# Layer 1: turned tiles in four PSUM banks where the experts' two are idle, in two elsewhere

## The chip, the cores and the metric

The kernel runs on one core of a Trainium2 chip. Its time is the device time in microseconds (us), the median of three runs. The engines are TensorE (PE; its weight loads are shown apart, as PEld), VectorE (DVE), ScalarE (ACT), GpSimd (POOL) and SyncE (SP), which issues transfers. PSUM, into which TensorE writes, is used here as eight banks of 128 partitions x 512 fp32 values.

## What is computed

Two transformer layers with adaptive layer norm on x of 8 x 512 x 128. Layer 0 is attention through landmarks with an iterated inverse, then a mixture of experts with capacity. The change lies in layer 1. Its part of the reference, cut:

```
h = _layernorm(x) * (1 + ca) + sa
# attention a = 0: 16 heads of 8, a bias by distance, gated
scores = einsum('bhqd,bhkd->bhqk', q, k) * scale + _tisa_bias(...)
attn = einsum('bhqk,bhkd->bhqd', softmax(scores), v)
a, g = split(attn @ w_gate + b_gate);  x = x + ga * (a * sigmoid(g))
h = _layernorm(x) * (1 + cb) + sb
# attention a = 1: causal, keys and values through a latent of 64
h = h + mla(rmsnorm(h, g1), Wq, Wdkv, Wuk, Wuv, Wo)
# 8 experts of 128 -> 256 -> 128, the two best weighted by a softmax
h = h + moe(rmsnorm(h, g2), gate_w, w1, w2)
x = x + gb * h
```

(The residual sums inside belong to the second block; each token's logits choose two experts, but all eight are computed.)

## The kernel before

**Tiles and steps.** Layer 1 works through 16 passes (`ORDER`): for each of the 8 sequences one pass of attention a = 0 and one causal pass a = 1, interleaved. A pass has 64 tiles, each 128 queries of one head against the keys: 512 of them for a = 0, and 128, 256, 384 or 512 for a = 1. The 1024 tiles (`ALL`) are software-pipelined: every engine runs one loop over steps m and does its part of a tile with a fixed lag. There is no scheduler; the order on each engine is what these loops write.

**A tile's way.** TensorE computes scores of tile m+2 into one of three banks (0 to 2, line 1723). VectorE adds bias or mask, negates and takes the minimum (line 1900, `X`, `nmax`; three buffers). GpSimd forms the difference to the row maximum (line 1583, `Y`; four buffers). TensorE turns tile m-3 of `Y` into a PSUM bank, one transpose per 128 keys (line 1737). ScalarE reads it from there through an exponential into `PT` (line 1625). Every fourth step TensorE multiplies four tiles of `PT` by the values into bank 5 (line 1752); the last column gives the sum for the softmax.

**Turned tiles and their slots.** Not only `Y` goes through the turned banks, but everything that TensorE makes for ScalarE to move: the output `O` of four heads (line 1762, every 16 steps), its turning for the projection (`turn`, 1766), the gate's two tiles (1772), the normalised rows (`xp`, `xm`, `xf`, 1778), projections (`pq`, `pk`, `mq` 1783; `ml` 1785; `mk` 1788) and values (`pv`, `mv` 1792). `turn_slots` numbers all 1200 of them in the order of the program, `SLOT[what]`. Slot c uses bank 3 + c % 2. Before TensorE writes one it waits until ScalarE has moved slot c - 2 (semaphore `moved`); ScalarE waits for `turned`. `moved` and `turned` count in slot order.

**The experts.** A round of experts (`moe`) runs beside the tiles for one sequence, at the steps `MOE_START[b]` and the 68 after: first the projection by Wo into bank `SIDE` (6), logits into bank `SIDE2` (7), then for each of 8 experts the hidden matmuls (line 1832) and the output ones (line 1846) in both banks; VectorE adds the outputs up (line 2095, semaphore `ye_added`). The rounds begin at steps 250, 378, 506, 634, 762, 890, 979 and 1043; the last one uses banks 0 to 2 for what comes before the outputs. Between rounds banks 6 and 7 are idle. The a = 0 passes are the first and those at odd places up to the 13th; nearly every one of them also carries the middle of a sequence (`mid`: gate, residual, two norms; on VectorE at places 22 to 36 of the pass).

**Waits.** TensorE works strictly in order: an instruction that waits holds up all behind it, so a transpose held by `moved` also holds the score matmul that VectorE needs next.

Of the kernel before, what the change touches and what calls it, by code (L numbers as in the profile page):

```python
# [13 lines left out]
B = 8  # L14
T = 512
# [9 lines left out]
E = 8  # L25
# [1215 lines left out]
TILES = H * TT  # L1241
# [5 lines left out]
ALL = len(ORDER) * TILES  # L1247
# [6 lines left out]
MOE_START = {b: TILES * PLACE[1, b + 1] - 6 for b in range(B - 2)}  # L1254
MOE_START[B - 2] = TILES * PLACE[1, B - 1] + MID_AT + 1
MOE_START[B - 1] = TILES * len(ORDER) + MID_AT + 1
HALVES = 2

STAGES = dict(wo=1, add=3, square=4, power=5, scale=7, turn=10, logits=12, read=14, top0=15, top1=16, gap=18,
              combine=20, first=12, each=6, second=2, tanh=1, mul=2, ye=9, half=2, sum=2)  # L1260
# [27 lines left out]
STEPS = MOE_START[B - 1] + done_at(B - 1) + 1  # L1288
# [1 line left out]
X_BUFS, Y_BUFS, PT_BUFS, W_BUFS, VW = 3, 4, 2, 3, HD + 2  # L1290
GATHER_AT, PRE_AT = 40, 2
T_LAG = 3
SIDE, SIDE2 = 6, 7


def tile_of(n):
# [8 lines left out]
def moe_at(m):  # L1305

    return [(b, m - first) for b, first in MOE_START.items() if 0 <= m - first <= done_at(b)]
# [7 lines left out]
def turned_at(s, i):  # L1315

    found = []
    if s < 0:
        return [("xp", 0), ("pq", 0), ("pk", 0), ("pv", 0)] if i == TILES - 1 else []
    if i % GROUP == 13 and 4 * s + i // GROUP >= 1 and 4 * s + i // GROUP <= 4 * len(ORDER):  # L1320
        found.append(("O", 4 * s + i // GROUP - 1))
    if i == MID_AT and 0 < s <= len(ORDER):
        found.append(("turn", s - 1))
    if s in MID_OF:
        found += [(name, MID_OF[s]) for at, name in ((19, "gate0"), (20, "gate1"), (38, "xm"), (40, "mq"), (41, "ml"),
                                                      (44, "mk"), (45, "mv")) if i == at]
    if s in PRE_OF:
        found += [(name, PRE_OF[s]) for at, name in ((10, "xp"), (21, "pq"), (23, "pk"), (25, "pv")) if i == at]
    found += [("xf", b) for b, k in moe_at(s * TILES + i) if k == stages(b)["turn"]]
    return found  # L1330


def turn_slots():

    slots = {}
    for m in range(-TILES, STEPS):
        if 0 <= m - T_LAG < ALL:
            slots["T", m - T_LAG] = len(slots)
        for what in turned_at(*divmod(m, TILES)):
            slots[what] = len(slots)  # L1340
    return slots


SLOT = turn_slots()


def layer1_phase(nc, sb_, sem, ps, x_sb, ident, half, mod_col, mods_dram, bias_dram, parts_dram, gate_keep,
# [4 lines left out]
    with local:  # L1352
# [79 lines left out]
        moved = sem("moved")  # L1432
# [17 lines left out]
        ye_added = sem("ye_added")  # L1450
# [20 lines left out]
        with nc.Block() as block:  # L1471
# [135 lines left out]
            def _(act):  # L1607
# [3 lines left out]

                def bank(what):
                    act.wait_ge(turned, SLOT[what] + 1)
                    return ps[:, 3 + SLOT[what] % 2, :]

                def move(n):
                    a, b, g, q, h = tile_of(n)
# [94 lines left out]
            def _(pe):  # L1712
# [11 lines left out]
                                     stack[:, 1, h, 0:keys(a, q)], start=True, stop=True).then_inc(scores_ready, 1)  # L1724

                def bank(what):
                    c = SLOT[what]
                    if c >= 2:
                        pe.wait_ge(moved, c - 1)
                    return 3 + c % 2  # L1730

                def transpose(n):
                    a, b, g, q, h = tile_of(n)
# [23 lines left out]
                def turn(name, k):  # L1757
# [34 lines left out]
                            last = nc.tensor.matmul(ps[:, to, t * C:(t + 1) * C], src[:, t * P:(t + 1) * P], w, start=True, stop=True)  # L1792
                    last.then_inc(turned, 1)

                def moe_side(b, i):
                    p = stages(b)
                    if i == p["wo"]:
                        if b == B - 1:
                            pe.wait_ge(shifted, ALL)
                        elif b:  # L1800
                            pe.wait_ge(ye_added, b * E * HALVES)
                        pe.wait_ge(moved, SLOT["turn", PLACE[1, b]] + 1)
                        for t in range(TT):
                            last = nc.tensor.matmul(ps[:, side_bank(b), t * C:(t + 1) * C], oT[1][:, t * P:(t + 1) * P], Wo_sb[:],
                                                    start=True, stop=True)
                        last.then_inc(mla_ready, 1)
                    if i == p["logits"]:
                        pe.wait_ge(moved, SLOT["xf", b] + 1)
                        for t in range(TT):
                            last = nc.tensor.matmul(ps[:, logits_bank(b), t * E:(t + 1) * E], fT[:, t * P:(t + 1) * P], gate_w_sb[:],  # L1810
                                                    start=True, stop=True)
                        last.then_inc(l1_logits, 1)
                    for e in range(E):
                        n = b * E + e
                        for f in range(FT1):
                            if i == hidden_at(b, e, f):
                                if f == 0:
                                    pe.wait_ge(experts_loaded[n % W_BUFS], (n // W_BUFS + 1) * 32)
                                if b == B - 1:
                                    if e == 0 and f == 0:  # L1820
                                        pe.wait_ge(mla_read, b + 1)
                                    elif e == 1 and f == 0:
                                        pe.wait_ge(logits_read, b + 1)
                                    elif e >= 1:
                                        pe.wait_ge(hid_evac, n * FT1 + f - 2)
                                elif e == 0:
                                    pe.wait_ge((mla_read, logits_read)[f], b + 1)
                                elif e == 1:
                                    pe.wait_ge(hid_evac, (n - 1) * FT1 + f + 1)
                                else:  # L1830
                                    pe.wait_ge(ye_added, (n - 2) * HALVES + f + 1)
                                nc.tensor.matmul(ps[:, hidden_bank(b, e, f), :], w1_e[:, n % W_BUFS, f * P:(f + 1) * P], fT[:],  # L1832
                                                 start=True, stop=True).then_inc(hid_ready, 1)
                        for u in range(HALVES):
                            if i == ye_at(b, e, u):
                                if u == 0:
                                    pe.wait_ge(hid_evac, (n + 1) * FT1)
                                if b == B - 1:
                                    pe.wait_ge(ye_added, (n - 1) * HALVES + u + 1)
                                elif e < E - 1:  # L1840
                                    pe.wait_ge(hid_evac, (n + 1) * FT1 + u + 1)
                                else:
                                    pe.wait_ge(ye_added, (n - 1) * HALVES + u + 1)
                                for t in (2 * u, 2 * u + 1):
                                    for f in range(FT1):
                                        last = nc.tensor.matmul(ps[:, SIDE + u, t * C:(t + 1) * C], hid[:, e % 2, f, t * P:(t + 1) * P],  # L1846
                                                                w2_e[:, n % W_BUFS, f, :], start=(f == 0), stop=(f == FT1 - 1))
                                last.then_inc(ye_ready, 1)
# [315 lines left out]
```

## Time and profile before

| | |
|---|---|
| median of three runs | 2079.36 us (2076.03 to 2079.79) |
| the profiled execution | 2073.5 us |
| its span, first to last instruction | 2071.5 us |
| TensorE busy, share of the span | 1779.4 us, 86% |
| its weight loads | 1306.9 us, 63% |
| VectorE | 1444.1 us, 70% |
| ScalarE | 1015.6 us, 49% |
| GpSimd | 857.9 us, 41% |
| granted clock of TensorE, mean over the span | 0.943 |

Layer 1's tiles run from 752 us to the end. Shares over the span mix layer 0 with layer 1, so the prediction reads single stretches. "Busy" adds up the shown durations; matmuls are pipelined, so TensorE's pace is better read from the starts of its instructions than from their lengths (a transpose of four matmuls has a shown length of 0.60 us, but the next instruction can start 0.44 us after it).

### The profile page before, as it was taken

What the parts mean: (1) busy time and instruction counts of PE and PEld (TensorE: products, weight loads), DVE (VectorE), ACT (ScalarE), POOL (GpSimd) and SP (SyncE); (2) the same over time, 40 slices, a digit from 0 to 9 for tenths busy, and PEclk for the clock granted to TensorE, in tenths of its full rate; (3) what the DMA queues carried; (4) which work ended last, traced back from release to release, by engine and by line L of the source; (5) the groups of instructions that cost most, each with busy time, mean ns of one, the idle gap of its engine ahead of it and who ended that gap; (6) DMA issues with size and microseconds to landing.
All of it is one profiled execution on the core that took longest, in us unless ns stands there. A gap on an engine that the chain in (4) does not pass through costs nothing.

```text
span 2071.5 us, 56863 instructions
## 1 busy us (share of the span) xinstructions
PE 1779.4 (86%) x21284; PEld 1306.9 (63%) x21284; DVE 1444.1 (70%) x4537; ACT 1015.6 (49%) x1992; POOL 857.9 (41%) x1253
## 2 busy tenths in 40 slices
PE   4485898898875729999999999999999999999997
PEld 2374677677763517766667666667666667766665
DVE  4574778876761127777787786787886887778765
ACT  1252544455441206666655654654654555655542
POOL 3500101110013017767655654655754663664530
PEclk7797999999996959999999999999999999999998
DMA  2512211222006411012013012012012112111211
GB/s 94 166 24 72 76 42 51 61 75 74 7 6 208 142 67 39 33 57 77 17 71 96 11 69 87 21 72 86 26 66 85 32 60 83 35 54 40 83 32 48
DMA packets 102694, 131.72 MB, mean 64 GB/s; under 512 B 14448, under 2 KB 87536, under 8 KB 101272
## 3 DMA queue, kind: packets, MB, share of 16 engines
q1 hardware_dynamic: 70600, 98.59, 14.6%
q10 hardware_dynamic: 28496, 18.10, 3.0%
q0 software_dynamic: 3328, 11.40, 1.7%
q8 instruction: 173, 2.83, 0.6%
q14 instruction: 97, 0.79, 0.1%
HBM read 100.05 MB, written 28.15 MB: 62 GB/s over the span
## 4 chain that ended last, share of the span: by engine, by line
PE 45%; DVE 8%; issue 6%; DMA 5%; POOL 2%; ACT 1%; ACTq 1%; SPq 1%; POOLq 0%; DVEq 0%
PE ps L1737 13%; PE ps L1752 7%; PE ps L1723 6%; PE ps L1846 5%; PE ps L1832 4%; DMA l_w_e<-in_L_ffn_w_dram 2%; DVE l_X L1900 2%; DMA l_stack<-parts_dram 2%; PE ps L1199 1%; POOL l_Y L1583 1%; PE ps L1208 1%; PE ps L1762 1%; PE ps L1783 1%; DVE l_xn L1931 1%; ACT PT L1625 1%
## 5 line engine op out<-in xcount | busy, mean ns | idle before, releaser
L1583 POOL TENSOR_SCALAR l_Y<-l_X,l_nmax 128x512 f32<-128x512 f32 (+3 forms) x1024 | 674.6, 664 | 521.1 <-PE ps L1737 286.0
L1625 ACT ACTIVATE PT<-ps 128x512 f32<-128x512 f32 (+3 forms) x1024 | 520.0, 517 | 405.8 <-PE ps L1737 356.3
L1737 PE MATMUL ps<-ident,l_Y 128*128 128x128 f32 x3328 | 549.7, 280 | 11.7 <-ACT PT L1625 7.7
L1737 PEld LDWEIGHTS ps<-ident,l_Y 128*128 128x128 f32 x3328 | 387.2, 142 | 195.3 <-issue 82.4
L1900 DVE CUSTOM_DVE_ANT_0 l_X<-ps,strips 128x512 f32<-128x512 f32 x512 | 342.1, 687 | 134.2 <-PE ps L1723 130.9
L1723 PE MATMUL ps<-l_stack 72*128 72x512 bf16 (+3 forms) x1024 | 351.0, 345 | 66.9 <-DVE l_nmax L1900 50.0
L1900 DVE CUSTOM_DVE_ANT_0 l_X<-ps,mask 128x384 f32<-128x384 f32 (+3 forms) x512 | 238.5, 485 | 41.0 <-PE ps L1723 35.6
L1752 PE MATMUL ps<-PT,v_aug 128*10 128x128 f32 x6656 | 230.1, 274 | 0.0
L1752 PEld LDWEIGHTS ps<-PT,v_aug 128*10 128x10 f32 x6656 | 156.8, 91 | 71.5 <-ACT PT L1625 42.6
L1723 PEld LDWEIGHTS ps<-l_stack 72*128 72x128 bf16 x1024 | 102.0, 100 | 102.6 <-DVE l_nmax L1900 77.3
L1832 PE MATMUL ps<-l_fT,l_w_e 128*128 128x512 f32 x256 | 138.9, 631 | 12.1 <-DMA l_w_e<-in_L_ffn_w_dram 9.3
L2084 DVE SCALAR_TENSOR_TENSOR l_hid<-l_hid,ps 128x512 f32<-128x512 f32 x128 | 87.7, 686 | 83.0 <-ACT l_hid L1689 81.6
L1846 PE MATMUL ps<-l_w_e,l_hid 128*128 128x128 f32 x1024 | 139.9, 281 | 3.1 <-DVE h_tok L2095 1.7
L1846 PEld LDWEIGHTS ps<-l_w_e,l_hid 128*128 128x128 f32 x1024 | 126.2, 192 | 21.7 <-issue 16.6
L512 POOL DMA_INDIRECT slots_in<-h,slot_all x32 | 32.4, 1014 | 230.3 <-DVE slot_all L1078 223.0
L1689 ACT ACTIVATE l_hid<-ps 128x512 f32<-128x512 f32 x128 | 76.3, 597 | 90.3 <-PE ps L1832 90.3
L668 PE MATMUL ps<-AV,Q 64*64 64x128 f32 (+1 forms) x1280 | 84.3, 289 | 36.0 <-DVE Q L1097 35.9
L480 POOL TENSOR_TENSOR rstd<-var_eps,half 128x4 f32<-128x4 f32 x16 | 17.8, 1111 | 232.3 <-DVE var_eps L864 232.3
L668 PE MATMUL ps<-X,AV 64*64 64x64 f32 x2560 | 93.1, 223 | 19.1 <-DVE X L1097 18.5
L2095 DVE SCALAR_TENSOR_TENSOR h_tok<-ps,combine,h_tok 128x128 f32<-128x128 f32 x256 | 77.3, 345 | 43.4 <-PE ps L1846 42.9
L668 PEld LDWEIGHTS ps<-X,AV 64*64 64x64 f32 x2560 | 82.7, 137 | 31.7 <-issue 16.4
L668 PEld LDWEIGHTS ps<-AV,Q 64*64 64x64 f32 x1280 | 74.6, 150 | 42.8 <-DVE Q L1097 40.0
(276 smaller groups left out, 2508.6 us busy)
## 6 DMA issues: line engine op xcount, KB each, us to landing
stack<-parts_dram SPq DMA_DIRECT2D x48, 384.0 KB
l_stack<-parts_dram SPq DMA_DIRECT2D x64, 288.0 KB
l_stack<-parts_dram SPq DMA_DIRECT2D x192, 96.0 KB
l_w_e<-in_L_ffn_w_dram ACTq DMA_DIRECT2D x128, 128.0 KB, 2.2
parts_dram<-l_parts SPq DMA_DIRECT2D x32, 384.0 KB, 2.5
strips<-bias_dram POOLq DMA_DIRECT2D x16, 448.0 KB, 11.2
parts_dram<-parts SPq DMA_DIRECT2D x16, 384.0 KB, 10.9
w_e<-in_L_ffn_w_dram SPq DMA_DIRECT2D x12, 256.0 KB, 5.7
```

The source lines that it names most:

```text
L668: last = nc.tensor.matmul(out(h), lhs(h), rhs(h), start=True, stop=True)
L1583: nc.gpsimd.tensor_scalar(Y[:, n % Y_BUFS, 0:w], X[:, n % X_BUFS, 0:w], -1.0, nmax[:, n % 8:n % 8 + 1], ALU.mult, ALU.add).then_inc(y_pool, 1)
L1625: nc.scalar.activation(dst, src, ACT.Exp).then_inc(moved, 1)
L1689: nc.scalar.activation(hid[:, e % 2, f, :], ps[:, hidden_bank(b, e, f), :], ACT.Tanh, scale=0.5).then_inc(hid_tanh, 1)
L1723: nc.tensor.matmul(ps[:, n % 3, 0:keys(a, q)], stack[:, 0, h, q * P:(q + 1) * P], stack[:, 1, h, 0:keys(a, q)], start=True, stop=True).the ...
L1737: last = nc.tensor.transpose(ps[:, to, k * P:(k + 1) * P], Y[:, n % Y_BUFS, k * P:(k + 1) * P], ident[:])
L1752: last = nc.tensor.matmul(ps[32 * j:32 * j + VW, 5, q * P:(q + 1) * P], v_aug[PLACE[a, b] % 2][:, k, h + j, :], PT[:, unit % PT_BUFS, j, k ...
L1832: nc.tensor.matmul(ps[:, hidden_bank(b, e, f), :], w1_e[:, n % W_BUFS, f * P:(f + 1) * P], fT[:], start=True, stop=True).then_inc(hid_read ...
L1846: last = nc.tensor.matmul(ps[:, SIDE + u, t * C:(t + 1) * C], hid[:, e % 2, f, t * P:(t + 1) * P], w2_e[:, n % W_BUFS, f, :], start=(f == ...
L1900: nc.vector.tensor_tensor_reduce(out=X[:, n % X_BUFS, 0:w], in0=ps[:, n % 3, 0:w], in1=add, scale=-1.0, scalar=3.0e38, op0=ALU.add, op1=AL ...
L2084: nc.vector.scalar_tensor_tensor(out=hid[:, e % 2, f, :], in0=hid[:, e % 2, f, :], scalar=1.0, in1=ps[:, hidden_bank(b, e, f), :], op0=ALU ...
L2095: last = nc.vector.scalar_tensor_tensor(out=h[:, t, :], in0=ps[:, SIDE + u, t * C:(t + 1) * C], scalar=combine[:, t, e:e + 1], in1=h[:, t, :],
```

## The change

Where no round of experts is active at the step or at any of the five steps behind it (`spare(m)`), a turned tile takes the least recently used of banks 3, 4, 6 and 7; elsewhere the least recently used of 3 and 4. `turn_slots` now also computes, for each slot, its bank, the slot that last used this bank, and for a tile in bank 6 or 7 the last round of experts before it. TensorE waits for the move of that earlier slot instead of the one two slots back, and for a tile in an experts' bank also until that round's sums are all added (`ye_added`). Ahead of a round's first write into bank 6 and bank 7 it waits until the last turned tile there has been moved (`turned_away`). ScalarE reads from the bank that the table names. VectorE, GpSimd and SyncE are not touched.

```diff
+def spare(m):
+
+    return 0 <= m < ALL and not any(moe_at(n) for n in range(m, m + 6))
+
+
 def turn_slots():
 
-    slots = {}
+    slots, banks, last = {}, [], {}
     for m in range(-TILES, STEPS):
-        if 0 <= m - T_LAG < ALL:
-            slots["T", m - T_LAG] = len(slots)
-        for what in turned_at(*divmod(m, TILES)):
-            slots[what] = len(slots)
-    return slots
-
-
-SLOT = turn_slots()
+        turns = [("T", m - T_LAG)] if 0 <= m - T_LAG < ALL else []
+        for what in turns + turned_at(*divmod(m, TILES)):
+            to = min((3, 4, SIDE, SIDE2) if spare(m) else (3, 4), key=lambda k: last.get(k, -1))
+            moes = [b for b in MOE_START if MOE_START[b] < m] if to in (SIDE, SIDE2) else []
+            banks.append((to, last.get(to), max(moes, default=None)))
+            last[to] = slots[what] = len(slots)
+    return slots, banks
+
+
+def side_use(m, k):
+
+    return max((SLOT[what] for what, at in TURN_AT.items() if at < m and BANKS[SLOT[what]][0] == k), default=None)
...
                 def bank(what):
                     act.wait_ge(turned, SLOT[what] + 1)
-                    return ps[:, 3 + SLOT[what] % 2, :]
+                    return ps[:, BANKS[SLOT[what]][0], :]
...
                 def bank(what):
-                    c = SLOT[what]
-                    if c >= 2:
-                        pe.wait_ge(moved, c - 1)
-                    return 3 + c % 2
+                    to, before, moe = BANKS[SLOT[what]]
+                    if before is not None:
+                        pe.wait_ge(moved, before + 1)
+                    if moe is not None:
+                        pe.wait_ge(ye_added, (moe + 1) * E * HALVES)
+                    return to
...
+                def turned_away(b, k):
+
+                    last = side_use(MOE_START[b], k) if b < B - 1 else None
+                    if last is not None:
+                        pe.wait_ge(moved, last + 1)
+
                 def moe_side(b, i):
                     p = stages(b)
                     if i == p["wo"]:
+                        turned_away(b, SIDE)
...
                         pe.wait_ge(moved, SLOT["xf", b] + 1)
+                        turned_away(b, SIDE2)
```

The order of instructions is the same on every engine. What differs is what they wait for. TensorE at the first steps after the first round of experts, in the kernel before, with the semaphores that each row waits for (`L1737` turns a tile, `L1723` computes scores, `L1752` multiplies by the values):

```order
2739 L1737 MATMUL ps<-ident,l_Y 128x128 [waits y_pool,moved]
2740 L1737 MATMUL ps<-ident,l_Y 128x128 x3
2741 L1723 MATMUL ps<-l_stack 128x512 [waits shifted]
2742 L1737 MATMUL ps<-ident,l_Y 128x128 [waits y_pool,moved]
2743 L1737 MATMUL ps<-ident,l_Y 128x128 x3
2744 L1723 MATMUL ps<-l_stack 128x512 [waits shifted]
2745 L1737 MATMUL ps<-ident,l_Y 128x128 [waits y_pool,moved]
```

Each turned tile waits for GpSimd's tile and for a move. The same place after the change (the lines are now 1753, 1737 and 1768):

```order
2739 L1753 MATMUL ps<-ident,l_Y 128x128 [waits y_pool,ye_added,moved]
2740 L1753 MATMUL ps<-ident,l_Y 128x128 x3
2741 L1737 MATMUL ps<-l_stack 128x512 [waits shifted]
2742 L1753 MATMUL ps<-ident,l_Y 128x128 [waits y_pool,ye_added,moved]
2743 L1753 MATMUL ps<-ident,l_Y 128x128 x3
2744 L1737 MATMUL ps<-l_stack 128x512 [waits shifted]
2745 L1753 MATMUL ps<-ident,l_Y 128x128 [waits y_pool,moved]
```

Nothing has moved. Two of every four tiles go to the experts' banks and wait for the experts' sums as well, and the `moved` of each row now asks for an older slot than before, which the view doesn't show.

## Rows read from the trace of the kernel before

**Rows 1.** Engine use by stretch: window, length, busy us (count) of each engine
```profile
core 0: us, PE busy (x) PEld busy (x) DVE busy (x) ACT busy (x) POOL busy (x), PEclk, DMA share, GB/s
916.10:971.60 55.50, 51.07 (x590) 33.71 (x590) 40.41 (x162) 33.65 (x77) 39.65 (x69) 1.00 0.22 80
1129.40:1193.60 64.20, 61.27 (x726) 43.35 (x723) 51.27 (x153) 40.15 (x69) 42.96 (x55) 1.00 0.08 24
1198.00:1292.80 94.80, 88.44 (x863) 63.29 (x861) 70.05 (x255) 46.57 (x102) 46.68 (x77) 0.96 0.24 80
1682.90:1773.20 90.30, 85.08 (x863) 61.73 (x861) 69.72 (x257) 46.15 (x102) 42.23 (x73) 1.00 0.24 81
```
**Rows 2.** Waits, 1129.4 to 1193.6: total us, times, longest
```profile
PEld ps L1737 <- ACT PT L1625: 5.1, 22, 0.5
```
**Rows 3.** Timeline, TensorE, 1141 to 1144: start, length, instruction [idle before <-releaser]
```profile
1141.16 0.60 PE L1737 MATMUL ps<-ident,l_Y 128*128 128x128 f32 x4
...
1141.60 0.38 PE L1723 MATMUL ps<-l_stack 72*128 72x512 bf16 x1
1141.79 0.42 PEld L1737 LDWEIGHTS ps<-ident,l_Y 128*128 128x128 f32 x4 [0.20 <-ACT PT L1625]
1141.82 0.63 PE L1737 MATMUL ps<-ident,l_Y 128*128 128x128 f32 x4
...
1142.29 0.38 PE L1723 MATMUL ps<-l_stack 72*128 72x512 bf16 x1
...
1142.51 0.60 PE L1737 MATMUL ps<-ident,l_Y 128*128 128x128 f32 x4
...
1143.14 0.66 PE L1762 MATMUL ps<-ident,l_O_sb 128*128 128x128 f32 x4
...
1143.63 0.38 PE L1723 MATMUL ps<-l_stack 72*128 72x512 bf16 x1
```
**Rows 4.** Timeline, TensorE, 1175 to 1186
```profile
1175.27 0.38 PE L1723 MATMUL ps<-l_stack 72*128 72x512 bf16 x1
...
1175.68 0.66 PE L1737 MATMUL ps<-ident,l_Y 128*128 128x128 f32 x4
...
1178.21 0.60 PE L1737 MATMUL ps<-ident,l_Y 128*128 128x128 f32 x4
...
1178.84 1.07 PE L1785 MATMUL ps<-l_hT,Wdkv_sb 128*64 128x512 f32 x2
...
1184.21 0.10 PEld L1723 LDWEIGHTS ps<-l_stack 72*128 72x128 bf16 x1 [0.76 <-DVE l_nmax L1900]
...
1184.96 0.66 PE L1762 MATMUL ps<-ident,l_O_sb 128*128 128x128 f32 x4
...
1185.73 1.16 PE L1792 MATMUL ps<-Wuv_sb,l_gated 64*128 64x128 f32 x8
```
**Rows 5.** Engine use within that stretch, 1154.4 to 1171.6
```profile
1154.40:1171.60 17.20, 15.33 (x206) 11.03 (x200) 16.99 (x56) 10.78 (x19) 12.74 (x14) 1.00 0.01 1
```
**Rows 6.** Timeline of the causal pass, TensorE and GpSimd, 919 to 956
```profile
919.61 0.27 PE L1723 MATMUL ps<-l_stack 72*128 72x256 bf16 x1
...
920.24 0.33 PE L1737 MATMUL ps<-ident,l_Y 128*128 128x128 f32 x1 [0.35 <-ACT PT L1625]
...
937.63 0.38 PE L1737 MATMUL ps<-ident,l_Y 128*128 128x128 f32 x2
...
938.25 1.13 PE L1783 MATMUL ps<-l_hT,w_in_sb 128*128 128x512 f32 x2 [0.24 <-ACT PT L1625]
...
954.64 1.72 POOL L1583 TENSOR_SCALAR l_Y<-l_X,l_nmax 128x384 f32<-128x384 f32 x3
...
955.37 0.52 PE L1737 MATMUL ps<-ident,l_Y 128*128 128x128 f32 x3 [0.27 <-ACT PT L1625]
```
**Rows 7.** Timeline at the end of the first round of experts, 1126 to 1130
```profile
1126.56 0.61 DVE L2095 SCALAR_TENSOR_TENSOR h_tok<-ps,combine,h_tok 128x128 f32<-128x128 f32 x2
...
1129.99 0.60 PE L1737 MATMUL ps<-ident,l_Y 128*128 128x128 f32 x4
```
**Rows 8.** One line's instructions: duration ns min/median/max, first and last start
```profile
L1735 PEldq EVENT_SEMAPHORE  x1024: 51/51/51, 754.0 to 2007.9; - x171
```

More of the change, by code:

```diff
@@ L1257 @@
 HALVES = 2
+SIDE, SIDE2 = 6, 7
 STAGES = dict(wo=1, add=3, square=4, power=5, scale=7, turn=10, logits=12, read=14, top0=15, top1=16, gap=18,
@@ L1292 @@
 T_LAG = 3
-SIDE, SIDE2 = 6, 7
 def tile_of(n):
@@ L1330, in turned_at @@
     return found
+def spare(m):
+    return 0 <= m < ALL and not any(moe_at(n) for n in range(m, m + 6))
 def turn_slots():
-    slots = {}
+    slots, banks, last = {}, [], {}
     for m in range(-TILES, STEPS):
-        if 0 <= m - T_LAG < ALL:
-            slots["T", m - T_LAG] = len(slots)
-        for what in turned_at(*divmod(m, TILES)):
-            slots[what] = len(slots)
-    return slots
-SLOT = turn_slots()
+        turns = [("T", m - T_LAG)] if 0 <= m - T_LAG < ALL else []
[7 more added lines that the diff above has]
+    return max((SLOT[what] for what, at in TURN_AT.items() if at < m and BANKS[SLOT[what]][0] == k), default=None)
+SLOT, BANKS = turn_slots()
+TURN_AT = {what: m for m in range(-TILES, STEPS)
+           for what in ([("T", m - T_LAG)] if 0 <= m - T_LAG < ALL else []) + turned_at(*divmod(m, TILES))}
 def layer1_phase(nc, sb_, sem, ps, x_sb, ident, half, mod_col, mods_dram, bias_dram, parts_dram, gate_keep,
```

## Prediction

> **What bounds the kernel now.** I began with the stretches in which the experts' two banks lie idle, since only there can the change act. In steps of the layer's main loop (one score tile each) they are 0 to 244, five stretches of 54 steps (319 to 372 and every 128th step from there), and 959 to 973: 530 of 1072 steps. The view of engine use by stretch gives their length [rows 1]: the stretch 1129.40 to 1193.60 is one of the five, 64.2 us for 54 steps, and TensorE is busy for 61.3 of it, VectorE for 51.3, ScalarE for 40.2. The reader is to see that TensorE is nearly full at full clock (2.4 GHz) and that ScalarE, which empties the turned banks, has a third of its time free. So banks can help only where a tile arrives at a bank whose reader is a fraction of a microsecond late.
>
> The view of waits for that stretch says how often that is: weight loads of the transposes waited 22 times for an exponential, 5.1 us in all [rows 2]. That is the upper end of what those waits could be worth there, and it is not what they cost: most of this idle time lies beside the score matmul that is still streaming. The timeline shows it [rows 3]. A transpose that isn't held starts 0.22 us after its score matmul (1141.60 to 1141.82) and the next score matmul follows 0.44 us later (1141.16 to 1141.60). The one whose weights came 0.20 us late (1141.79) also starts after 0.22, and only the next score matmul comes late, at 0.47 instead of 0.44. A wait shown as 0.20 costs 0.03.
>
> **The change, part by part.** No instruction moves on any engine and none is added but waits. What changes is which earlier tile a turned tile waits for: its bank's last reader was two slots back, and is now four back in the idle stretches (608 of the 1200 turned tiles; 14 more are the first in their bank for a long time).
>
> *A stretch of 54 steps.* I went down TensorE's timeline and took each start against the shortest distance seen for the same pair.
> 1. Ordinary tiles: each fourth transpose loses 0.03 [rows 3]; there are 13 in the stretch, 3 of them while another engine sets the pace (below). 10 x 0.03 = 0.3.
> 2. The turned output tile (line 1762) starts 0.63 behind the transpose (1142.51 to 1143.14) where 0.44 does, and takes 0.49 to the next score matmul instead of 0.44 [rows 3]: 0.24. Of three in a stretch, this one counts in full, one falls in VectorE's part, the third (1184.96) loses 0.13, to its start and after it.
> 3. The second gate tile and the two projections from the normalised rows stand 0.63 behind a transpose as well; the row at 1178.84 stands for the three [rows 4]: 3 x 0.19 = 0.57. A fourth one counts nothing: the score matmul after it (1184.21) waited for VectorE.
> 4. The transpose at 1175.68 stands 0.41 behind its score matmul where 0.22 does, and loses 0.05 more after it: 0.24 [rows 4]. One more such transpose, before the first gate tile, counts nothing, since that gate tile needs the data which ScalarE was moving.
> 5. The value projection (1185.73) stands 0.77 behind the output tile where 0.44 does: 0.33 [rows 4].
> The sum is 0.3 + 0.24 + 0.13 + 0.57 + 0.24 + 0.33 = 1.81 us.
>
> What doesn't count: between 1154.40 and 1171.60 VectorE is busy for 16.99 of 17.20 us [rows 5]. TensorE's gains there vanish in its wait for scores to be read. Gains ahead of that part count, since VectorE was waiting for TensorE when it began, and gains after it count too. Five stretches give 5 x 1.81 = 9.1 us; steps 192 to 244 are the same work: 1.8.
>
> *Steps 0 to 126.* Forty-odd steps of plain work (10 x 0.03, three output tiles at 0.24, so 1.0), then one round like the stretch above with one more output tile: 2.1. Together 3.1 us.
>
> *The causal pass, steps 127 to 191* (916.10 to 971.60), has short tiles, so one late reader weighs more [rows 1, 6]. The transpose at 920.24 stands 0.63 behind its score matmul where 0.11 would do: it waits for the exponential of a 512-wide tile two slots back. That is 0.5, and 0.05 after it. The projection at 938.25 stands 0.62 behind a transpose of two tiles where 0.22 does: 0.4. Added up in this way, the tiles to 942 give 3.6 us; I left out what precedes 925.5, where normalised rows had to be waited for anyway. After that GpSimd sets the pace in part: at 954.64 it begins three tiles that take 0.57 each, and the transpose at 955.37 needs the first of them. Of 2.2 us of waits there I keep 1.0. Sum 4.6; with none of it kept 0, with all of it 6.6. I take the middle since ahead of 942 the inputs of these transposes lay ready for over a microsecond.
>
> *Steps 959 to 973* start like the causal pass: 1.4 us (0 to 1.6).
>
> *What is added.* After the first round of experts, 173 tiles that go to an experts' bank carry a third wait, for the experts' last sum. It costs in two ways. The sum itself: its last pair of operations begins at 1126.56 [rows 7] and lasts 0.61, and the first tile that needs it starts at 1129.99, so there are 2.8 us to spare; I price it at nothing, and no more than 0.3 per stretch if TensorE arrived that much earlier. The waiting instruction: all 1024 transposes already have one wait as an instruction of its own, 0.051 us each [rows 8], and still start 0.22 behind the score matmul [rows 3], so one is hidden. A second one is shown nowhere; hidden it costs 0, wholly exposed 173 x 0.051 = 8.8 us. I take 0, as the queue has the 0.44 us of each transpose to work ahead. The waits ahead of the experts' own matmuls ask for a tile at least six steps old: nothing.
>
> The Trainium skill bears on this last point ("Perfetto Trace Analysis", Identifying Dependency Chains): further waits are put as EventSemaphore instructions ahead of the one that needs them. The rows agree on the form, and say nothing of the price of a second.
>
> **The sum.** 9.1 + 1.8 + 3.1 + 4.6 + 1.4 = 20.0 us off. The profiled execution took 2073.5 us (its span 2071.5, 2.0 around it), so 2053.5 for such a one. The median of the runs shown is 2079.36, 5.9 above it, and 2059.4 by the same subtraction. Between the stretches the experts' rounds stay as they are, bound by TensorE, VectorE and the weights' transfers, and shift earlier as a whole: their transfers are issued behind their own matmuls, not by the clock. The forecast's own bounds: 14 us off (nothing from both causal parts) to 24.
>
> **Rivals.**
> *The second waiting instruction is exposed*, or transposes that are no longer held meet the next late thing (values waiting for the exponential six steps back). For: in the causal pass the step is so short that 0.10 us of waiting instructions is most of it, and the matmuls with the values wait for the same exponentials. Against: ScalarE is a third idle. With 8.8 us lost, 11 off remain: 2068.
>
> *VectorE takes it all.* It is busy for 80% of the stretch [rows 1], and if the score matmuls' waits for it grew by what the banks give, nothing is left: 0 to 3 us off, 2078. Against: in the stretch it waits for TensorE before and after its full part.
>
> *More comes off than the pairs show*, since an earlier score matmul also ends VectorE's stalls sooner, in both causal parts above all: 27 off, 2052.
>
> *The other side: the clock.* In the experts' rounds the granted clock averages 1.00 where the round takes 90.3 us, and 0.96 where it takes 94.8 [rows 1]: a fall from 2.4 to 1.2 GHz for some microseconds, behind a wait for weights, went with up to 4.5 us. If four banks broke TensorE's work up so that the clock fell in the idle stretches too, say twice in each of the five, ten falls at 4.5 us are 45, 25 more than the gain: 2104. It decides from five falls on. Against it: the gaps only shrink, and the mean over the stretches is 1.00.
> The Trainium skill has this very rule ("TensorE: Matmul & The Clock Gate", A second HAM failure mode: psum-queue depth-cycling): a kernel that cycled through PSUM banks left TensorE idle for short moments so often that its clock went up and down. Here two banks are cycled through already and the rows show the full clock, so I give it little.
>
> *The change doesn't do what it says*, if the least recently used bank were always 3 or 4; the slots as computed put 314 tiles into the experts' banks, so no.
>
> **How the numbers follow.** Forecast (14 to 24 off) 0.60; exposed waits (5 to 14 off) 0.18; VectorE takes it all 0.10; more than 24 off 0.06; the clock, slower 0.05; other 0.01. The range leaves out the clock, most of VectorE's case and the far end of the large gain: 2051 to 2073. A measurement of this kernel can tell about 0.2%, 4.2 us, from no change. Faster by more: the first, second and fourth, 0.84; within: 0.11; slower: 0.05.
>
> **What would show it.** In the profile after, the stretch of 54 steps should last 62.4 instead of 64.2 and the causal pass some 51; TensorE's weight loads should hardly wait for line 1625's exponentials in the stretches; output tiles should stand 0.44 behind a transpose; ScalarE's waits for TensorE stay. If tiles with a third wait start later than 0.22 behind the score matmul while their neighbours don't, the second wait is exposed. If waits of the score matmuls for VectorE grow by what the transposes lose, VectorE took it. I am wrong in size if an experts' round grows, and in kind if the clock falls within a stretch.

## The result, and the profile after

The changed kernel takes 2050.54 us (median of 6 runs, 2050.42 to 2057.22); the kernel before, run beside it, 2077.15 us (6 runs, 2071.38 to 2079.79). The ratio is 0.9883, with a 95% interval of 0.9864 to 0.9903, which is some 24 us off; the two medians are 26.6 apart. The profiled spans are 2071.5 and 2048.6, 22.9 apart. Faster, as forecast, with the time just below the low end of the range, 2051. The forecast's 20.0 off is a ratio of 0.9904, at the upper end of this interval; run again on another occasion, the changed kernel took 2060.66 against 2079.7, ratio 0.9905 (0.9886 to 0.9925).

Cut at the starts of VectorE's reads of the score tiles, the two profiled executions compare as follows. Where no profile row stands beside it, a time below comes from this same cut of a trace.

| steps | before, us | after, us | off | forecast off |
|---|---|---|---|---|
| ahead of step 0 (layer 0 and the loads) | 752.4 | 750.4 | 2.0 | 0 |
| 0 to 21 | 41.92 | 41.72 | 0.20 | } 1.0 |
| 22 to 63 | 45.96 | 44.05 | 1.91 | } |
| 64 to 126 | 73.22 | 71.10 | 2.12 | 2.1 |
| 127 to 191, causal pass | 58.15 | 55.30 | 2.85 | 4.6 |
| 192 to 244 | 63.45 | 61.38 | 2.07 | 1.8 |
| the five stretches of 54 | 5 x 64.2 | 5 x 62.15 | 10.4 | 9.1 |
| 959 to 978 | 14.35 | 12.94 | 1.41 | 1.4 |
| the six experts' rounds | 580.89 | 580.43 | 0.46 | 0 |

The stretches in which the change acts give 20.9 us, where 20.0 were forecast; the table is of one execution each. The misses of the single rows cancel in part: 1.1 and 1.3 us more than forecast in steps 0 to 63 and in the five stretches, 1.8 less in the causal pass. The 2.0 us ahead of step 0 aren't the change's: that point lay at 752.4 in this execution of before and at 750.4, 761.0 and 757.7 in three executions of kernels with an identical first part. The end, behind the last step, is 0.5 longer. In steps 0 to 21 there was little to gain: their first 28 us ran at 1.2 GHz in every kernel here (the granted clock was 0.50 from 752.40 to 780.50 before), and within them VectorE waited 20.3 us for a transfer of modulation values (`gb_now`), with TensorE behind it.

Engine use by stretch, of after (columns as in [rows 1]): the causal pass with the wait ahead of it (58.15 before, steps 127 to 191 of the table; without that wait, as in [rows 1], it lasts 52.0 instead of 55.5, where some 51 were forecast), a stretch of 54 steps, the first round of experts and the fifth.

```profile
core 0: us, PE busy (x) PEld busy (x) DVE busy (x) ACT busy (x) POOL busy (x), PEclk, DMA share, GB/s
907.30:962.60 55.30, 49.83 (x628) 35.77 (x621) 41.19 (x167) 33.34 (x79) 40.77 (x71) 1.00 0.25 84
1121.50:1183.60 62.10, 59.07 (x726) 45.06 (x724) 51.04 (x153) 39.71 (x69) 43.05 (x55) 1.00 0.08 25
1028.80:1122.00 93.20, 86.35 (x862) 62.78 (x862) 69.52 (x255) 45.82 (x101) 45.84 (x76) 0.98 0.24 81
1663.10:1753.60 90.50, 84.87 (x862) 61.86 (x857) 69.56 (x255) 45.59 (x102) 41.51 (x72) 1.00 0.24 80
```

The second row answers to 1129.40:1193.60 in [rows 1]. The work is the same: 726 matmuls, and VectorE busy for 51.0 us against 51.3. TensorE's busy time fell from 61.3 to 59.1 as well, since a transpose that was held is shown as 0.63 or 0.66 us long [rows 3, 4] and one that wasn't as 0.60. So it isn't the idle share that shows the gain (2.9 and 3.0 us) but the length. The waits of that stretch, first after and then before (what waits for what: us in all, times, longest):

```profile
DVE l_X L1924 <- PE ps L1737: 10.7, 14, 1.5
PEld ps L1737 <- DVE l_nmax L1924: 5.1, 4, 1.8
PE ps L1737 <- DVE l_nmax L1924: 3.0, 2, 1.6
PEld ps L1753 <- issue: 2.8, 13, 0.2
PEld ps L1753 <- ACT PT L1639: 0.7, 2, 0.3
```

```profile
DVE l_X L1900 <- PE ps L1723: 12.6, 15, 1.5
PEld ps L1723 <- DVE l_nmax L1900: 4.8, 5, 1.8
PE ps L1723 <- DVE l_nmax L1900: 2.5, 2, 1.6
```

The row of [rows 2], 22 waits and 5.1 us of weight loads for exponentials, is down to 2 waits and 0.7 us. The whole stretch became 2.07 us shorter. VectorE's wait for scores fell by 1.9; the waits of the score matmuls for VectorE grew by 0.3 on their weight loads and by 0.5 on the matmuls themselves.

TensorE's timeline after, the place of [rows 3] (start, length, instruction):

```profile
1133.58 0.38 PE L1737 MATMUL ps<-l_stack 72*128 72x512 bf16 x1
1133.80 0.60 PE L1753 MATMUL ps<-ident,l_Y 128*128 128x128 f32 x4
1134.24 0.38 PE L1737 MATMUL ps<-l_stack 72*128 72x512 bf16 x1
1134.45 0.60 PE L1753 MATMUL ps<-ident,l_Y 128*128 128x128 f32 x4
1134.89 0.60 PE L1778 MATMUL ps<-ident,l_O_sb 128*128 128x128 f32 x4
1135.33 0.38 PE L1737 MATMUL ps<-l_stack 72*128 72x512 bf16 x1
```

Every transpose is now 0.44 from its start to the next score matmul, the fourth too (1133.80 to 1134.24, before 0.47). The output tile starts 0.44 behind the transpose (before 0.63) and the score matmul 0.44 behind it (before 0.49). Both values are those that the forecast named.

### The profile page after: what moved, and what is told of

Same layout as the page of the kernel before. It is cut to its first block, busy times and chain, and to the rows that moved or that the text cites. A ratio compares the mean times of both kernels' runs of the same rounds, so it can differ in the third digit from the quotient of the medians.

```text
span 2048.6 us, 56879 instructions
## 1 busy us (share of the span) xinstructions
PE 1752.8 (86%) x21284; PEld 1319.2 (64%) x21284; DVE 1440.9 (70%) x4537; ACT 1009.5 (49%) x1992; POOL 857.7 (42%) x1253
## 4 chain that ended last, share of the span: by engine, by line
PE 46%; DMA 7%; DVE 6%; issue 4%; POOL 2%; ACT 1%; SPq 1%; ACTq 1%; POOLq 0%; DVEq 0%
PE ps L1753 14%; PE ps L1768 8%; PE ps L1737 6%; PE ps L1870 5%; PE ps L1856 4%; DMA l_stack<-parts_dram 3%; DMA l_w_e<-in_L_ffn_w_dram 2%; POOL l_Y L1597 2%; PE ps L1199 1%; PE ps L1208 1%; PE ps L1778 1%; DVE l_X L1924 1%; PE ps L1799 1%; DMA parts_dram<-l_parts 1%; PE ps L1808 1%
## 5 line engine op out<-in xcount | busy, mean ns | idle before, releaser
L1753 PE MATMUL ps<-ident,l_Y 128*128 128x128 f32 x3328 | 542.8, 278 | 9.9 <-ACT PT L1639 6.8
L1753 PEld LDWEIGHTS ps<-ident,l_Y 128*128 128x128 f32 x3328 | 402.3, 142 | 166.0 <-issue 82.6
L1737 PE MATMUL ps<-l_stack 72*128 72x512 bf16 (+3 forms) x1024 | 350.9, 345 | 74.1 <-DVE l_nmax L1924 55.2
L1737 PEld LDWEIGHTS ps<-l_stack 72*128 72x128 bf16 x1024 | 101.3, 99 | 111.3 <-DVE l_nmax L1924 81.9
```

Source lines behind the costliest of these rows:

```text
L1737: nc.tensor.matmul(ps[:, n % 3, 0:keys(a, q)], stack[:, 0, h, q * P:(q + 1) * P], stack[:, 1, h, 0:keys(a, q)], start=True, stop=True).the ...
L1753: last = nc.tensor.transpose(ps[:, to, k * P:(k + 1) * P], Y[:, n % Y_BUFS, k * P:(k + 1) * P], ident[:])
```

## Experiments

Each edit is made on the changed kernel, and each run stands beside runs of the kernel before on the same chip: one set of 13 (median 2084.49) for the first four, one of 15 (2079.7) for the others. Profiled stretches are compared most, since the five stretches of 54 steps of one execution lie within 0.06 us, save where the clock fell.

### Two banks again, but the experts' own

```diff
-            to = min((3, 4, SIDE, SIDE2) if spare(m) else (3, 4), key=lambda k: last.get(k, -1))
+            to = min((SIDE, SIDE2) if spare(m) else (3, 4), key=lambda k: last.get(k, -1))
```

> In the idle stretches turned tiles alternate between the experts' two banks only, and leave banks 3 and 4 alone; depth two as in the kernel before, but every tile in those stretches after the first round carries the third wait. Theory (what pays is the distance to the bank's last reader, and a satisfied third wait is hidden): no gain at all, each stretch of 54 steps 64.2 us as before, ratio to before 0.999 to 1.001. Rival (third wait exposed, 0.05 us each on some 350 tiles): 10 to 17 us slower than before, stretches near 67. Rival (banks 6 and 7 are themselves better than 3 and 4): stretches near 62.1.

Ratio 0.9996 (0.9975 to 1.0018). Engine use, a stretch of 54 steps and the causal pass:

```profile
1142.90:1207.10 64.20, 61.26 (x724) 43.31 (x723) 51.26 (x153) 40.22 (x69) 43.14 (x55) 1.00 0.08 24
928.20:983.70 55.50, 51.01 (x590) 33.62 (x588) 40.31 (x163) 33.76 (x77) 39.90 (x69) 1.00 0.23 80
```

These are the lengths of before, 64.2 and 55.5 [rows 1]. All moved tiles carry the third wait here, and nothing is lost by it (what form that wait takes stands at the next experiment). Which banks are used counts for nothing; how many tiles back the bank's last reader stands is all.

### The third wait only once in a round

```diff
-            banks.append((to, last.get(to), max(moes, default=None)))
+            moe = max(moes, default=None)
+            banks.append((to, last.get(to), moe if moe not in seen else None))
+            seen.add(moe)
```

> The change, but the wait for the experts' sums stands only ahead of the first tile in an experts' bank after each round, so some 165 waiting instructions are gone. Theory (they were hidden): within 1 us of the changed kernel, stretches 62.1 us, ratio to before 0.988. Rival (each costs 0.05 us): stretches 60.9 us and 8 us less than the changed kernel in all.

Ratio 0.9882 (0.9844 to 0.9921). The same stretch:

```profile
1127.60:1189.70 62.10, 59.06 (x723) 45.05 (x724) 51.04 (x153) 39.76 (x69) 43.26 (x55) 1.00 0.08 25
```

62.1, as after. All but six of the 173 extra waits are gone, and not 0.1 us with them. That doesn't price a second waiting instruction, though, since there hardly is one. By line, in after:

```profile
L1745 PEldq EVENT_SEMAPHORE  x10: 51/51/51, 1141.8 to 1805.0; - x10
L1751 PEldq EVENT_SEMAPHORE  x1022: 51/51/51, 774.4 to 1984.5; - x171
```

L1745 is the wait for the experts' sums, L1751 the one for GpSimd's tile that each transpose had before too [rows 8]. Of the 173 waits for the sums only ten became an instruction of their own, ahead of the first gate tile and of one projection in each of the five stretches. The trace shows the other 163 as a second semaphore of a waiting instruction that was there already, 143 of them on L1751, which lasts 51 ns with one semaphore or two. So this run and the one with two banks show that asking for the sums costs nothing; the ten instructions would be 0.5 us in all if wholly exposed, and the stretches are equal without them, 62.1 us each.

### Three banks

```diff
-            to = min((3, 4, SIDE, SIDE2) if spare(m) else (3, 4), key=lambda k: last.get(k, -1))
+            to = min((3, 4, SIDE) if spare(m) else (3, 4), key=lambda k: last.get(k, -1))
```

> The change with three banks (3, 4, 6) in the idle stretches instead of four. Theory (a bank's reader is late by less than one exponential, 0.65 us): nearly all of the gain, stretches 62.1 to 62.3 us; the causal pass loses at most 0.5 of its 2.8 us; ratio to before 0.988 to 0.990. Rival (a reader can be late by two moves): half of the gain or less, stretches above 63.0.

Ratio 0.9873 (0.9832 to 0.9914).

```profile
1129.00:1191.10 62.10, 59.06 (x723) 45.06 (x724) 51.03 (x155) 39.76 (x69) 43.09 (x55) 1.00 0.08 25
917.93:970.20 52.27, 48.37 (x589) 33.95 (x588) 39.88 (x162) 32.68 (x77) 39.56 (x69) 1.00 0.25 84
```

The third bank brings all of the gain in the stretch. The fourth adds some 0.4 us in the causal pass and 0.2 in steps 959 to 973 (9.36 against 9.15), each of them from one profiled execution with three banks: the readers are late by part of a tile, not by two.

### No spare banks where VectorE is full

```diff
+    s, i = divmod(m, TILES)
+    if s in MID_OF and 21 <= i < 38:
+        return False
```

> The change, but in places 21 to 37 of the passes that carry the middle of a sequence, where VectorE is full, turned tiles keep to banks 3 and 4. Theory (what TensorE gains there is lost in its wait for VectorE): the same time as the changed kernel, each stretch of 54 steps 62.1 to 62.3 us, ratio to before 0.988. Rival (a good part of the 2.1 us per stretch comes from there, as waits ahead of VectorE's part feed it): stretches 62.6 us or more, 4 us in all.

Ratio 0.9875 (0.9836 to 0.9915).

```profile
1127.10:1189.20 62.10, 59.46 (x726) 44.58 (x724) 51.02 (x153) 39.94 (x69) 42.96 (x55) 1.00 0.08 25
```

The length is that of after, 62.1, while TensorE is busy 0.4 us longer: what the banks give between these steps is waited away.

### The spare banks in the causal parts alone

```diff
-    return 0 <= m < ALL and not any(moe_at(n) for n in range(m, m + 6))
+    return (127 <= m < 192 or 959 <= m < ALL) and not any(moe_at(n) for n in range(m, m + 6))
```

> Four banks only in the causal parts without a round (steps 127 to 191 and 959 on), two everywhere else. Theory (each stretch's gain stands by itself): steps 127 to 192 take 55.2 us as in the changed kernel (58.1 before), 959 to 979 1.4 us less, all other stretches as before (64.2 each); 4.3 us off in all, ratio to before 0.998. Rival (a gain in one stretch is taken back in the next, or feeds it): 192 to 245 or 250 to 319 move by over 0.5 us beyond what a fall of the clock does.

Ratio 0.9985 (0.997 to 1.0). A stretch of 54 steps, then the causal pass:

```profile
1132.40:1196.60 64.20, 61.26 (x726) 43.32 (x723) 51.27 (x153) 40.19 (x69) 42.99 (x55) 1.00 0.08 24
922.70:974.50 51.80, 47.77 (x589) 34.13 (x588) 39.90 (x162) 32.19 (x77) 39.61 (x69) 1.00 0.25 84
```

All other stretches have the lengths of before, to 0.05. The profile's idle stretches sum to 4.4 us less (609.61 against 614.04). So the gains belong to their places, with one exception: with the wait ahead of it the causal pass lasts 54.72 us here, and 55.14 to 55.30 in four executions with four banks that gain ahead of it as well. Some 0.5 us of what is gained ahead is lost there, at a transfer (see the causal pass below).

### One bank

```diff
-            to = min((3, 4, SIDE, SIDE2) if spare(m) else (3, 4), key=lambda k: last.get(k, -1))
+            to = min((3,) if spare(m) else (3, 4), key=lambda k: last.get(k, -1))
```

> One bank only (3) in the idle stretches, for the other end of the scale. Theory (a tile waits for its bank's last reader, here the exponential of the tile just before): in plain steps a transpose can start only when that exponential, which starts at its end, is over, so a step takes some 0.65 for the exponential and 0.6 for the transposes up to their landing, 1.3 us instead of 0.95, and the stretches of 54 steps 80 to 85 us instead of 64.2; in all 150 to 190 us slower. Rival (TensorE's order hides part of it behind score and value matmuls): under 75 us per stretch.

2496.16 us, one run, 416 more than before and far more than was expected. Engine use in two stretches of 54 steps, and TensorE's timeline at either level of the clock:

```profile
1315.80:1421.00 105.20, 80.22 (x723) 47.26 (x719) 52.36 (x154) 40.50 (x69) 40.52 (x56) 0.87 0.06 18
1520.40:1628.90 108.50, 84.14 (x721) 47.98 (x719) 52.00 (x154) 40.50 (x69) 39.40 (x56) 0.83 0.05 18
```

```profile
1332.76 0.38 PE L1737 MATMUL ps<-l_stack 72*128 72x512 bf16 x1
1333.61 0.66 PE L1753 MATMUL ps<-ident,l_Y 128*128 128x128 f32 x4 [0.47 <-ACT PT L1639]
1334.10 0.38 PE L1737 MATMUL ps<-l_stack 72*128 72x512 bf16 x1
...
1411.41 1.11 PE L1753 MATMUL ps<-ident,l_Y 128*128 128x128 f32 x4 [0.26 <-ACT PT L1639]
```

At full clock the transpose stands 0.85 behind its score matmul instead of 0.22, and a tile takes 1.34 us (1332.76 to 1334.10). That much was the theory. On top of it TensorE's clock fell: from step 22 on, 295 us of the idle stretches ran at 1.2 GHz, the granted clock averages 0.87 and 0.83 above, and four transposes then take 1.11 instead of 0.60 to 0.66. So the rival of the clock is a real mechanism of this kernel, at the other end of the scale. It isn't all of the miss: some 27 us of the stretch of 105.2 were at the low level (0.87), and if everything took twice as long in them, 91.6 would be left at full clock (an estimate), still above the 80 to 85 expected. Where the rest comes from wasn't worked out. With two, three and four banks, the nine profiled executions have four falls in the idle stretches, each of a few microseconds. The stretch at step 703 took 63.75 us with one, instead of 62.15, and a fall in the causal pass also cost 1.6; one inside VectorE's full part cost nothing (62.15). The forecast's price of 4.5 us for a fall was too high here.

### The spare banks for longer

```diff
+def banks_at(m):
+    if not 0 <= m < ALL:
+        return (3, 4)
+    side = not any(moe_at(n) for n in range(m, m + 3))
+    active = [(b, first) for b, first in MOE_START.items() if first <= m + 6 and m <= first + done_at(b)]
+    side2 = not active or (len(active) == 1 and active[0][0] < B - 1 and m <= active[0][1] + 10)
+    return (3, 4) + (SIDE,) * side + (SIDE2,) * side2
```

> Banks 6 and 7 are used for longer: bank 6 up to the third step ahead of a round, bank 7 up to the tenth step of it (the logits need it at the twelfth), with the wait for the experts' sums once per round. Theory (a tile held by its bank costs TensorE what it starts late, wherever TensorE sets the pace): steps 245 to 259 of each of the six rounds lose one output tile's 0.24, two or three ordinary tiles' 0.03, and at steps 257 and 260 0.3 and 0.5: about 1.2 us per round, 7 us in all, a ratio to before of 0.984 to 0.986. Rival (the experts' rounds are set by VectorE, the weights' transfers and the clock): rounds 554 us in sum as now, and the same time as the changed kernel.

Ratio 0.9894 (0.9867 to 0.9921); after, run again beside it, 0.9905 (0.9886 to 0.9925). No difference; the 7 us of the theory didn't come. The first steps of an experts' round do gain: in the third round (from step 506) TensorE is 0.8 us ahead of after (run again) at its best, and 0.5 once it has turned the round's normalised rows. Then comes the second hidden matmul of the round's first expert, first in this kernel and then in after, run again:

```profile
1373.91 1.55 DVE L1967 TENSOR_SCALAR l_xn<-x_sb,l_mean_var,l_rstd 128x128 f32<-128x128 f32 x4 [0.76 <-POOL l_rstd L1600]
1375.38 0.18 DVE L2078 COPY l_logit<-ps 128x32 f32<-128x32 f32 x1
1375.61 1.13 PE L1868 MATMUL ps<-l_fT,l_w_e 128*128 128x512 f32 x2 [0.71 <-DVE l_logit L2078]
```

```profile
1370.37 0.18 DVE L2066 COPY l_logit<-ps 128x32 f32<-128x32 f32 x1
1370.60 1.12 PE L1856 MATMUL ps<-l_fT,l_w_e 128*128 128x512 f32 x2
```

It waits for VectorE's copy of the logits, which stands behind the normalised rows, which wait for GpSimd's reciprocal root. That chain came no sooner with more banks, and at this matmul TensorE loses 0.8 us and stands 0.3 behind after. In five of the six rounds the lead is gone in this way by the round's 18th step, and in the sixth by its 30th. This shows why the first steps of a round have nothing to give; the rest of a round has no more banks here and wasn't tested.

> The changed kernel once more, so that the next ones are compared with it on one chip. Both theories: idle stretches 593 us in sum, 20.7 less than before; the experts' rounds 555 us plus or minus 3, by how often the clock falls in them; ratio to before 0.988.

The second look at after gave the lengths of the first to 0.1 us in every idle stretch.

## Why the prediction was right, and where its steps were off

**The mechanism** holds. "A wait shown as 0.20 costs 0.03" was exact: each fourth transpose gave 0.03. The Trainium skill says of such a pattern ("Perfetto Trace Analysis", Optimization Strategy) that the same gap repeating on the engine that should be saturated can mean that there isn't enough PSUM for the next tile. The trace agrees, but the size of the gap is no measure of it: the transposes' 5.1 us of them [rows 2] fell by 4.4, and the stretch, other turned tiles and all, became 2.07 shorter.

**The time itself** came out below the range, and not by what the range was made of. In the profiled executions, 2050.5 us was measured where 2053.5 was forecast: 0.9 of the 3.0 between them is the change's, 2.0 lie ahead of step 0. The medians differ by 26.6, which the prediction gave 0.06 as "more than 24 off", for VectorE's stalls ending sooner in the causal parts. The causal parts gave less than forecast, so that rival isn't what happened: the change's own 20.9 lie within the 14 to 24, and the rest is how far executions of one kernel lie apart (run again, the medians differed by 19.0). That 20.9 lies so near 20.0 is in part luck, since the misses below cancel.

**A stretch of 54 steps: 1.81 forecast, 2.07 measured.** By item, from the starts on TensorE in both traces, which sum to 2.13 (forecast, measured): ordinary tiles 0.3, 0.20; output tiles 0.24 and 0.13, 0.25 and 0.08; second gate tile with two projections 0.57, 0.68; transpose at 1175.68 0.24, 0.25; value projection 0.33, 0.24. Two steps failed. First, what was counted at nothing: the transpose ahead of the first gate tile, and that gate tile, gave 0.34, though the tile "needs the data which ScalarE was moving", and the fourth projection gave 0.10. Second, a projection that is released late also lasts longer to the next score matmul, 0.96 where 0.86 does; I had counted only the 0.19 ahead of it. TensorE at the place of [rows 4], after:

```profile
1167.20 0.60 PE L1753 MATMUL ps<-ident,l_Y 128*128 128x128 f32 x4
1167.64 1.02 PE L1799 MATMUL ps<-l_hT,Wq_sb 128*128 128x512 f32 x2
1168.50 0.38 PE L1737 MATMUL ps<-l_stack 72*128 72x512 bf16 x1
1168.72 0.60 PE L1753 MATMUL ps<-ident,l_Y 128*128 128x128 f32 x4
1169.25 1.07 PE L1801 MATMUL ps<-l_hT,Wdkv_sb 128*64 128x512 f32 x2
...
1175.19 0.60 PE L1778 MATMUL ps<-ident,l_O_sb 128*128 128x128 f32 x4
1175.72 1.16 PE L1808 MATMUL ps<-Wuv_sb,l_gated 64*128 64x128 f32 x8
```

The first projection stands 0.44 behind its transpose and is 0.86 long to the next score matmul. The second (its weights have 64 columns) and the value projection (64 rows) stay at 0.53, free bank or not. That is why the value projection gave 0.24 and not 0.33; what the last 0.09 is, no run here tells.

**In VectorE's part nothing stays**, as forecast: TensorE gains 0.69 us from step 341 to 352 and loses 0.70 at step 353, to its waits for scores to be read. The experiment without spare banks there says the same.

**Steps 22 to 63: 1.0 forecast for all up to 63, 2.1 measured.** The step that failed is "plain work (10 x 0.03, three output tiles at 0.24)". There are three projections there, at steps 21 to 25, each of the kind above. Before, then after:

```profile
797.73 0.60 PE L1737 MATMUL ps<-ident,l_Y 128*128 128x128 f32 x4
798.36 1.13 PE L1783 MATMUL ps<-l_hT,w_in_sb 128*128 128x512 f32 x2
799.32 0.38 PE L1723 MATMUL ps<-l_stack 72*128 72x512 bf16 x1
```

```profile
795.23 0.60 PE L1753 MATMUL ps<-ident,l_Y 128*128 128x128 f32 x4
795.66 1.02 PE L1799 MATMUL ps<-l_hT,w_in_sb 128*128 128x512 f32 x2
796.52 0.38 PE L1737 MATMUL ps<-l_stack 72*128 72x512 bf16 x1
```

0.63 became 0.43 and 0.96 became 0.86: 0.3 us each, 0.9 for the three, which is the whole difference within 0.2.

**The causal pass: 4.6 forecast, 2.85 measured.** This term was over-sized by 1.8, and hid the misses above in the sum. Part of it lies where I hadn't looked, ahead of the pass. Its first score matmul, before and after:

```profile
915.84 0.23 PE L1723 MATMUL ps<-l_stack 72*128 72x128 bf16 x1 [0.80 <-DMA l_stack<-parts_dram]
```

```profile
910.25 0.23 PE L1737 MATMUL ps<-l_stack 72*128 72x128 bf16 x1 [1.44 <-DMA l_stack<-parts_dram]
```

It waits for the transfer that brings the queries' and keys' parts back from memory. The score matmul ahead of it had come 6.24 us earlier in the span than before, and this one only 5.59, so 0.65 us was given back at once. Where nothing was gained ahead (spare banks in the causal parts alone) that matmul comes 2.89 us behind the one before it, as in before (2.76), against 3.2 to 3.4 in six executions of kernels that gain ahead. From that matmul on, the pass gave 3.5: 2.9 up to where I kept 3.6, and 0.6 of the 1.0 that I had kept behind it. The prediction contradicts itself on these 3.6: it says that it leaves out what precedes 925.5, and names the transpose at 920.24 as a gain. By the starts, 2.6 us were gained from 925.5 to 942 and none of it was lost; ahead of 925.5 single gains of 1.2 came and 0.9 went again. Only both together (3.7) make the 3.6, so the part that was to be left out seems to stand in it. Single gains come as forecast (the transpose of 920.24 [rows 6] 0.51 and 0.05, the projection of 938.25 0.41 and 0.10), and others go back into waits for GpSimd and VectorE. Two of them, after:

```profile
916.80 1.00 POOL L1588 TENSOR_TENSOR l_rstd<-l_var_eps,half 128x4 f32<-128x4 f32 x1
...
918.42 0.41 PE L1753 MATMUL ps<-ident,l_Y 128*128 128x128 f32 x2 [0.53 <-POOL l_Y L1597]
...
940.13 0.23 PE L1737 MATMUL ps<-l_stack 72*128 72x128 bf16 x1 [1.01 <-DVE l_nmax L1924]
```

The first stood at 0.23 before (924.33): GpSimd's reciprocal root lies between, and it hangs on statistics. The reason that I gave for the middle value, "the inputs of these transposes lay ready for over a microsecond", holds for a transpose by itself; of the 0.9 us gained from the pass's first score matmul to step 132, 0.3 were left at step 138. Whether more of VectorE's and GpSimd's buffers would keep these gains wasn't tried.

**The third wait: 0 forecast, 0 measured**, but not for the reason given. The prediction took it for 173 further waiting instructions ("wholly exposed 173 x 0.051 = 8.8 us") that are hidden; ten were added, and the rest share an instruction that was there. So the rival of 8.8 us rested on instructions that don't exist, and what a second one in a row ahead of a transpose costs stays open.

**The experts' rounds stay as they are** only in their sum. Singly they differ by up to 3.3 us between these two executions (the first: 90.0 before, 93.2 after), with the clock: 1.00 for 90.5 and 0.98 for 93.2 above. Rounds of before and after without a fall in them agree within 0.3. The total time at a clock below full in the rounds was 13.7 us before and 6.8 after, and 6.8 to 17.1 in the other runs with two banks or more. The rounds' sum lies between 576.4 and 583.0 in the nine executions, so a difference of 0.46 us says nothing.

**The clock** didn't fall in any idle stretch of the first profile after. The Trainium skill's rule on it ("TensorE: Matmul & The Clock Gate", A second HAM failure mode: psum-queue depth-cycling) is about short idle moments when cycling through banks. Such moments, with falls of the clock, show here with one bank, where most ordinary tiles wait 0.47 us. With two, three and four banks, all of them cycled through, the stretches ran at full clock but for the four falls above. So in this kernel cycling by itself isn't what does it. The prediction's "the mean over the stretches is 1.00" doesn't hold for the first 28 us from step 0, which every kernel ran at the low level.

## What to carry to other kernels

A displayed wait of a weight load under a streaming matmul is nearly free; read the distance between two starts against the shortest that the same pair reaches anywhere, behind the late one as well as ahead of it, and do so for every form in every stretch, the "plain" ones too. One bank more than the reader's lateness asks for is enough: two to three gave all in the long tiles, the fourth 0.6 us in all. In a part where several engines run close together, follow the gain on through the next transfer and the next chain of statistics before you keep it: pairwise gaps gave 4.6 us and 2.85 came. Before you price added waits by the waiting instruction, count such instructions: 173 waits added ten.

## What the runs showed of the hardware

- A transpose held by its bank costs by what it overlaps: 0.20 us of wait was 0.03 behind a 512-wide score matmul, 0.19 and 0.06 or 0.10 behind another turned tile, and 0.5 behind a 256-wide one.
- One waiting instruction on TensorE's queue lasts 51 ns, with one semaphore to wait for (879 on L1751) or with two (143). With one ahead of nearly every transpose (1022 of 1024), a transpose that isn't held still starts 0.22 us behind its score matmul. A second one in a row ahead of a transpose was run nowhere.
- With one bank TensorE's clock spent 295 us of the idle stretches from step 22 on at 1.2 GHz; in such a stretch the engine is shown as busy for 80.2 of 105.2 us. With two banks or more it was at 2.4 GHz there in all but a few microseconds. The first 28 us from step 0 ran at 1.2 GHz with any number of banks.
- Busy time of TensorE isn't work: it fell by 2.2 us in a stretch with the same 726 matmuls.
